# Unread products on TensorE beside the attention units of two lone bodies: the first image's first attention and the last image's second

## The chip, the cores and the metric

The kernel runs on one core of one Trainium2 chip. The metric is the device time of the whole program in microseconds (us); lower is better. What the profile calls PE is TensorE, DVE is VectorE, ACT is ScalarE, POOL is GpSimd, and SP is SyncE, which here only issues plain DMAs. A difference below about 0.5% (23 us) can't be told from no change in this kernel.

## The reference, cut to what matters

Thirty-two images, each of 384 tokens (256 image patches and 128 text tokens) of width 192, go through two layers. Each layer is an attention and a mixture of experts, both with a residual.

```python
h = concat(patch_embedding(x), text_embedding(x_txt))          # 32 x 384 x 192
h = h + L0_attn(layernorm(h))      # 12 heads of 16, softmax, two kinds of queries, values normalised per head
h = h + L0_ffn(layernorm(h))       # 5 experts, all computed, 2 of them weighted in
h = h + L1_attn(layernorm(h))      # 6 heads of 32, causal, low-rank projections
h = h + L1_ffn(layernorm(h))       # 8 experts, each takes up to a fixed number of tokens of the whole batch
```

The change adds nothing to what is computed: its products go to a PSUM bank that nobody reads.

## The kernel before

The program has two stages. `token_stages` takes the images one after the other through everything up to the choice of experts of the second layer. `expert_stage` then runs the eight experts over the tokens of all images. The change touches only the first one.

**Streams and bodies.** The work of one image is cut into four streams: w (embedding and first norm), x (first attention), y (first mixture of experts), z (second attention, and the places of the tokens in the expert buffers). `units()` gives each stream a list of units. The images are pipelined: a body r works on stream w of image r, x of image r-1, y of image r-2 and z of image r-3. `active[r]` says which streams a body has: "w", "wx", "wxy", then "wxyz" for 29 bodies, and at the end "xyz", "yz", "z". So the body "wx" holds the first attention of the first image with no expert work beside it, only a few units of w. The body "z" holds the second attention of the last image, alone. In all the bodies between, products of y stand between the units of attention.

**Order.** `schedule()` merges the streams by strings of letters, `ORDER` and `ORDER_OF_ONE`, and drops units of streams that a body doesn't have. All five engines run through the same list of units, each issuing what is its own; semaphores join them. All is unrolled.

**Units of an attention k** (k = 0 in x, k = 1 in z). "qk" projects a tile of 128 tokens. DVE, POOL and ACT rotate the result and split it into a high and a low part (`parts`). "blocks" transposes the parts on PE (12 transposes) and ACT and DVE copy them to `heads_t`. "maxima" computes two heads' products for one tile of queries in two banks of `bank_v`; DVE reduces each to its row maximum (`neg_max`, L1104). "shift" transposes the maxima and ACT writes them into a row of `heads_t`. "score" computes two heads' shifted scores in two banks of `bank_a`; ACT takes their exponential into `probs` (L760). "apply" multiplies `probs` by the values into `bank_o[k]`, four heads side by side for k = 0, two for k = 1. "sums" and the rest follow.

There are three banks `bank_a`, three `bank_v`, and two `bank_o`, one for each attention. Before it fills a bank, PE waits in `fill_a` or `fill_v` until the bank's last content was read. A first attention has 3 units of blocks, 18 of maxima, 18 of scores and 9 of apply, 48 in all. A second has 3, 9, 9 and 9, 30 in all.

At the start SP also clears `xs_dram` by 29 large DMAs, and POOL gathers the rows of the next image's text tokens (`rows_in`) by indirect DMAs, issued in the unit "rows"; POOL adds the gathered rows into `h[0]` in "patches", and DVE waits for that in the unit "stats" of stream w.

`w_ffn` holds gate and up weights of the first layer's experts as F32R; it is written before the bodies start and isn't changed after.

Of the kernel before, what the change touches and what calls it, by code (L numbers as in the profile page):

```python
# [14 lines left out]
P = 128  # L15
# [198 lines left out]
def token_stages(nc, consts, img, txt, seg, curve, projw, projb, tok_table, seg_table, wqkv,  # L214
# [5 lines left out]
    with ctx:  # L220
        def sb(name, shape, dt=F32):
            return ctx.enter_context(nc.sbuf_tensor(name, shape, dt))

        def ps(name):
            return ctx.enter_context(nc.psum_tensor(name, [P, 512], F32))
# [18 lines left out]
        w_ffn = sb("w_ffn", [P, 3, 2 * E0 * I0 + 8], F32R)  # L244
# [90 lines left out]
        bank_o = [ps(f"bank_o{i}") for i in range(2)]  # L335
# [175 lines left out]
        def body(active, image_w, image_z, fill=()):  # L511
# [58 lines left out]
            with nc.Block(no_gpsimd_drain=True) as block:  # L570
# [209 lines left out]
                def _(pe):  # L780
# [85 lines left out]
                    def apply(k, g, kt):  # L866
# [11 lines left out]
                                           start=(kt == 0), stop=(kt == NT - 1))  # L878
                        mm.then_inc(applied, 1)

                    for r, what, *at in order:
                        if what == "patches":
                            pe.wait_ge(own_ready, nth["w"][r] + 1)
                            for t in range(2):
                                pe.matmul(fill_v("patch", t)[:, 0:D], patches_t[:, t, :], own_proj[:],
                                          start=True, stop=True).then_inc(v_full, 1)
# [16 lines left out]
                        elif what == "qk":  # L903
# [5 lines left out]
                            else:  # L909
# [3 lines left out]
                                          stop=True).then_inc(v_full, 1)  # L913
# [46 lines left out]
                        elif what == "logits":  # L960
# [7 lines left out]
                            for t in range(NT):  # L968
# [4 lines left out]
                                for n, (xb, wb) in enumerate(products):  # L973
                                    mm = pe.matmul(o, ffn_x[:, xb, tile[t]], w_ffn[:, wb, router_cols],
                                                   start=(n == 0), stop=(n == len(products) - 1))
                            mm.then_inc(v_full, 1)
                        elif what == "ffn":
                            e, m = at
                            for name, fill, full in (("gate", fill_a, a_full), ("up", fill_v, v_full)):
                                bank = fill(name, e, m)  # L980
                                first = ffn_cols[name == "up"].start + e * I0 + m * P
                                for n, (xb, wb) in enumerate(products):
                                    mm = pe.matmul(bank[:, 0:T], w_ffn[:, wb, first:first + P], ffn_x[:, xb, :],  # L983
                                                   start=(n == 0), stop=(n == len(products) - 1))
                                mm.then_inc(full, 1)
                        elif what == "down":
                            e, = at
                            pe.wait_ge(hid_ready, hid_nth(r, e, 1) + 1)
                            for t in range(NT):
                                bank = fill_v("down", e, t)  # L990
                                for m in range(2):
                                    mm = pe.matmul(bank[:, 0:D], hid[:, e % 2, m, tile[t]], w_down[:, m, e, :],  # L992
                                                   start=(m == 0), stop=(m == 1))
                                mm.then_inc(v_full, 1)
                        elif what == "low_rank":
                            halves_ready("xt", 2)
                            for w, bank, rows, full in ((w_a, fill_a("r_qk"), 64 + RANK, a_full),
                                                        (w_va, fill_v("r_v"), RANK, v_full)):
                                for half in range(2):
                                    mm = pe.matmul(bank[0:rows, 0:T], w[:, half, :], xt[2][0:KH, half, :],  # L1000
                                                   start=(half == 0), stop=(half == 1))
# [653 lines left out]
```

## Time and profile before

| what | value |
|---|---|
| median of 3 runs | 4603.84 us (4586.52, 4603.84, 4605.22) |
| profiled execution, device time | 4596.28 us |
| its span in the trace | 4594.5 us |
| PE busy over the span | 4277.7 us (93%) |
| DVE, ACT, POOL busy | 62%, 49%, 51% |
| mean granted clock of TensorE | 0.949 of full |

How to read it. The span is the time from the first to the last record of the profiled execution; 1.8 us of its device time lie outside. The granted clock is 1.00 at 2.4 GHz and 0.50 at 1.2 GHz; a stretch with a number between the two has both levels in it. A row of the timeline gives the start and the length of a group of instructions; the length counts to the end of the last one, so the step from one start to the next is what a group costs in a row of work. In brackets stands how long the engine sat idle before the row, and who released it.

### The profile page before, as it was taken

How to read it: one execution, taken by the hardware profiler on the slowest of the kernel's cores; microseconds unless marked ns; L12 is line 12 of the kernel's file. 1: busy time of each engine (PE TensorE's matmuls, PEld its weight loads, DVE VectorE, ACT ScalarE, POOL GpSimd, SP SyncE). 2: the span in 40 equal slices, each digit the busy share in tenths (PEclk: the TensorE clock that was granted, in tenths of full speed). 3: DMA queues.
4: the chain of work that ended last, by engine and by line, in shares of the span. 5: the costliest groups of instructions: out<-in, count | busy, mean ns of one | idle time of the engine just before them, and what ended most of it. 6: DMA issues, size and time to landing. Idle time of an engine off the chain costs nothing. (4 is left out here: it accounts for less than half of the span.)

```text
span 4594.5 us, 77772 instructions
## 1 busy us (share of the span) xinstructions
PE 4277.7 (93%) x26706; PEld 3303.2 (72%) x26706; DVE 2864.9 (62%) x8055; ACT 2257.5 (49%) x5154; POOL 2361.8 (51%) x2439
## 2 busy tenths in 40 slices
PE   2799999999999999999999999999999699999999
PEld 1566666766666666666666667666666489999999
DVE  4476777777777767676767677676775333333333
ACT  1455555555555555555555555555554233333333
POOL 2345555555555555555555555555553245555555
PEclk8799999999999999999999999999999799999999
DMA  8500000000000000000000000000000022222221
GB/s 161 93 8 10 16 9 12 9 12 10 11 11 11 11 11 13 8 13 10 15 11 13 9 12 9 12 9 12 11 9 9 16 70 48 64 74 64 72 63 21
DMA packets 158998, 122.08 MB, mean 27 GB/s; under 512 B 63807, under 2 KB 150358, under 8 KB 158614
## 3 DMA queue, kind: packets, MB, share of 16 engines
q1 hardware_dynamic: 123990, 80.19, 8.1%
q0 software_dynamic: 34624, 36.92, 3.1%
q8 instruction: 223, 3.65, 0.3%
q14 instruction: 161, 1.32, 0.1%
HBM read 76.75 MB, written 74.58 MB: 33 GB/s over the span
## 5 line engine op out<-in xcount | busy, mean ns | idle before, releaser
L760 ACT ACTIVATE probs<-bank_a 128x384 f32<-128x384 f32 (+2 forms) x1728 | 692.0, 453 | 671.0 <-PE bank_a L857 425.8
L1104 DVE TENSOR_REDUCE neg_max<-bank_v 128x1 f32<-128x352 f32 (+3 forms) x1728 | 777.2, 491 | 198.2 <-PE bank_v L832 107.0
L652 POOL TENSOR_SCALAR gate_tanh<-gate_tanh 128x384 f32<-128x384 f32 x320 | 382.2, 1195 | 679.9 <-ACT gate_tanh L777 677.1
L832 PE MATMUL bank_v<-heads_t 50*128 50x352 f32 (+4 forms) x1728 | 402.0, 401 | 77.3 <-DVE neg_max L1104 55.0
L875 PE MATMUL bank_o<-probs,v 128*32 128x384 f32 (+3 forms) x3456 | 441.6, 481 | 4.0 <-ACT sums_t L765 0.3
L832 PEld LDWEIGHTS bank_v<-heads_t 50*128 50x128 f32 (+1 forms) x1728 | 215.1, 194 | 301.3 <-DVE neg_max L1104 142.7
L857 PE MATMUL bank_a<-heads_t 50*128 50x384 f32 (+3 forms) x1728 | 388.2, 386 | 45.3 <-ACT probs L760 38.7
L619 POOL TENSOR_TENSOR rstd<-ve,pow_half 128x3 f32<-128x3 f32 x128 | 113.8, 889 | 578.0 <-DVE ve L1043 576.0
L1406 POOL DMA_INDIRECT out_tokens<-res,token x232 | 230.9, 995 | 331.8 <-DVE res L1592 281.8
L983 PE MATMUL bank_a<-ffn_x,w_ffn 128*128 128x384 f32 x1600 | 389.9, 377 | 0.0
L992 PE MATMUL bank_v<-w_down,hid 128*128 128x192 f32 x1920 | 365.2, 342 | 3.1 <-DVE h_y L1260 1.4
L983 PE MATMUL bank_v<-ffn_x,w_ffn 128*128 128x384 f32 x1600 | 355.7, 355 | 0.0
L654 POOL TENSOR_TENSOR hid<-gate_tanh,hid 128x384 f32<-128x384 f32 x320 | 331.4, 1036 | 33.0 <-DVE hid L1249 7.3
L749 ACT ACTIVATE heads_t<-bank_a 1x384 fp32r<-1x384 f32 x576 | 277.5, 482 | 136.3 <-PE bank_a L845 128.6
L992 PEld LDWEIGHTS bank_v<-w_down,hid 128*128 128x128 f32 x1920 | 318.9, 196 | 35.2 <-issue 31.2
L1585 DVE TENSOR_TENSOR e_hid<-e_bank_v,gated 128x384 f32<-128x384 f32 (+1 forms) x320 | 173.4, 544 | 263.2 <-PE e_bank_v L1471 261.2
L857 PEld LDWEIGHTS bank_a<-heads_t 50*128 50x128 f32 (+1 forms) x1728 | 211.8, 192 | 173.5 <-ACT probs L760 113.5
L1471 PE MATMUL e_bank_a<-split_t,w_in 128*128 128x384 f32 (+1 forms) x1600 | 332.5, 338 | 2.7 <-DVE split_t L1540 2.7
L1249 DVE TENSOR_TENSOR hid<-bank_v,half_gate 128x384 f32<-128x384 f32 x320 | 177.4, 554 | 240.5 <-PE bank_v L983 197.4
L1471 PE MATMUL e_bank_v<-split_t,w_in 128*128 128x384 f32 (+1 forms) x1600 | 325.3, 333 | 0.0
L1442 PE MATMUL e_bank_a<-w_out,e_hid 128*128 128x192 f32 x1856 | 314.8, 326 | 0.5 <-DVE e_hid L1585 0.5
L983 PEld LDWEIGHTS bank_a<-ffn_x,w_ffn 128*128 128x128 f32 x1600 | 286.0, 203 | 39.0 <-issue 24.2
(227 smaller groups left out, 8934.2 us busy)
## 6 DMA issues: line engine op xcount, KB each, us to landing
xs_dram<-zeros SPq DMA_DIRECT2D x29, 780.0 KB, 19.4
rows<-xs_dram SPq DMA_DIRECT2D x232, 96.0 KB
out_tokens<-h_z SPq DMA_DIRECT2D x32, 288.0 KB, 2.3
rows<-xs_dram SPq DMA_DIRECT2D x232, 33.5 KB
raw<-in_w SPq DMA_DIRECT2D x8, 512.0 KB, 3.9
raw<-in_w SPq DMA_DIRECT2D x16, 256.0 KB, 5.2
sofar<-out_tokens,token POOLq DMA_INDIRECT x232
out_tokens<-res,token POOLq DMA_INDIRECT x232
```

The costliest lines, as they stand in the source:

```text
L652: step(pool.tensor_scalar(gate_tanh[:, m, :], gate_tanh[:, m, :], 1.0, None, ALU.add))
L654: pool.tensor_tensor(hid[:, e % 2, m, :], gate_tanh[:, m, :], hid[:, e % 2, m, :], ALU.mult).then_inc(hid_ready, 1)
L749: ins = act.activation(heads_t[k][to:to + 1, b, :], bank[at:at + 1, 0:T], ACT.Copy)
L760: act.activation(probs[:, n % NPROBS, i, lo:T], empty("score", k, g, kt, i)[:, lo:T], ACT.Exp, scale=DHS[k] ** -0.5).then_inc(a_free, 1)
L832: mm = pe.matmul(bank[:, 0:keys], heads_t[k][r:r + rows, b, tile[t]], heads_t[k][r:r + rows, 6 + b, 0:keys], start=True, stop=(k == 0))
L857: mm = pe.matmul(bank[:, lo:T], heads_t[k][at:at + rows, 6 + b, tile[kt]], heads_t[k][at:at + rows, b, lo:T], start=True, stop=(k == 0))
L875: mm = pe.matmul(bank_o[k][i * rows:(i + 1) * rows, lo:T], v[:, kt, PER_GROUP[k] * g + i, :], probs[:, probs_of[r, k, g, kt] % NPROBS, i, ...
L983: mm = pe.matmul(bank[:, 0:T], w_ffn[:, wb, first:first + P], ffn_x[:, xb, :], start=(n == 0), stop=(n == len(products) - 1))
L992: mm = pe.matmul(bank[:, 0:D], hid[:, e % 2, m, tile[t]], w_down[:, m, e, :], start=(m == 0), stop=(m == 1))
L1104: dve.tensor_reduce(neg_max[k][g % 2][:, t, at:at + 1], bank[:, 0:keys], AX.X, ALU.max, negate=True).then_inc(v_free, 1)
L1442: mm = pe.matmul(bank[:, 0:D], hid[:, ch % 2, m, t * P:(t + 1) * P], w_out[ch // NCHUNK % 2][:, m, :], start=(m == 0), stop=(m == NM - 1))
L1471: mm = pe.matmul(bank[:, 0:width], w[:, wb, at:at + P], x[:, xb, 0:width], start=(n == 0), stop=(n == 4))
```

## The change

Ahead of each unit blocks, maxima, score or apply, in the bodies "wx" and "z" alone, PE issues one or two products of a 128 x 128 weight block of `w_ffn` and 512 columns of `w_ffn`, into the one of the two `bank_o` that belongs to the other attention. Two stand ahead of each unit in "wx", one in "z". They wait for nothing, signal nothing, and stand ahead of the unit's own waits.

```diff
+                    def keep_busy(times):
+                        spare = bank_o["z" not in active[r]]
+                        for _ in range(times):
+                            pe.matmul(spare[:], w_ffn[:, 0, 0:P], w_ffn[:, 0, 0:512], start=True, stop=True)
+
                     for r, what, *at in order:
+                        if active[r] in ("wx", "z") and what in ("blocks", "maxima", "score", "apply"):
+                            keep_busy(2 if "x" in active[r] else 1)
                         if what == "patches":
```

What stands in a row on PE in the body "wx", one step of the first attention (apply, two units of maxima, two of scores, apply). L875 is apply, L832 maxima, L857 scores. Before:

```order
L875 MATMUL bank_o0<-probs,v0 32x384 x4
L832 MATMUL bank_v1<-heads_t0 128x352
L832 MATMUL bank_v2<-heads_t0 128x352
L832 MATMUL bank_v0<-heads_t0 128x384
L832 MATMUL bank_v1<-heads_t0 128x384
L857 MATMUL bank_a1<-heads_t0 128x384
L857 MATMUL bank_a2<-heads_t0 128x384
L857 MATMUL bank_a0<-heads_t0 128x384
L857 MATMUL bank_a1<-heads_t0 128x384
L875 MATMUL bank_o0<-probs,v0 32x384 x4
```

The same place on PE after; L884 is the new line.

```order
L875 MATMUL bank_o0<-probs,v0 32x384 x4
L884 MATMUL bank_o1<-w_ffn 128x512 x2
L832 MATMUL bank_v1<-heads_t0 128x352
L832 MATMUL bank_v2<-heads_t0 128x352
L884 MATMUL bank_o1<-w_ffn 128x512 x2
L832 MATMUL bank_v0<-heads_t0 128x384
L832 MATMUL bank_v1<-heads_t0 128x384
L884 MATMUL bank_o1<-w_ffn 128x512 x2
L857 MATMUL bank_a1<-heads_t0 128x384
L857 MATMUL bank_a2<-heads_t0 128x384
L884 MATMUL bank_o1<-w_ffn 128x512 x2
L857 MATMUL bank_a0<-heads_t0 128x384
```

Nothing changes place; five pairs of products come into each such step. In all, 48 pairs stand in the body "wx".

PE in the body "z", one step of the second attention (maxima, score, apply; L838 and L863 add the causal mask), after; before, the same rows stand there without L884.

```order
L884 MATMUL bank_o0<-w_ffn 128x512
L832 MATMUL bank_v0<-heads_t1 128x256
L832 MATMUL bank_v1<-heads_t1 128x256
L838 MATMUL bank_v0<-maskq,identb 128x128
L838 MATMUL bank_v1<-maskq,identb 128x128
L884 MATMUL bank_o0<-w_ffn 128x512
L857 MATMUL bank_a1<-heads_t1 128x256
L857 MATMUL bank_a2<-heads_t1 128x256
L863 MATMUL bank_a1<-maskt,identb 128x128
L863 MATMUL bank_a2<-maskt,identb 128x128
L884 MATMUL bank_o0<-w_ffn 128x512
L875 MATMUL bank_o1<-probs,v1 64x384 x2
```

Here too nothing moves; 30 single products are added. DVE, ACT, POOL and SP have the same instructions in the same order as before.

## Rows read from the trace of the kernel before

**Rows 1.** Stretch: its length, busy PE PEld DVE ACT POOL, PEclk, DMA

```profile
145.00:150.00 5.00, 4.37 (x21) 3.83 (x19) 2.88 (x8) 0.97 (x2) 0.00 (x0) 0.52 1.12 168
```

**Rows 2.** Stretches: the body "wx" from 101 on, then two in body "z"

```profile
101.00:145.00 44.00, 31.57 (x138) 11.59 (x139) 12.53 (x28) 21.01 (x47) 3.52 (x5) 0.50 1.15 174
...
3605.00:3610.00 5.00, 4.97 (x9) 1.88 (x9) 2.33 (x7) 1.46 (x5) 3.08 (x4) 0.50 0.00 0
...
3625.00:3630.00 5.00, 4.88 (x27) 2.59 (x25) 1.78 (x4) 1.98 (x6) 0.00 (x0) 0.70 0.00 0
```

**Rows 3.** What PE waited for, 101 to 145: total us, times, longest

```profile
PE bank_v L832 <- DVE neg_max L1104: 7.3, 6, 3.8
PE bank_a L857 <- ACT probs L760: 6.6, 9, 1.0
PE bank_a L857 <- ACT heads_t L749: 1.1, 1, 1.1
```

**Rows 4.** Timeline of PE in "wx": start, length, line, what [idle before, releaser]

```profile
121.12 0.66 PE L832 MATMUL bank_v<-heads_t 50*128 50x352 f32 x2 [0.74 <-DVE neg_max L1104]
121.55 0.55 PE L857 MATMUL bank_a<-heads_t 50*128 50x384 f32 x2
122.80 0.69 PE L857 MATMUL bank_a<-heads_t 50*128 50x384 f32 x2 [0.70 <-ACT probs L760]
123.42 1.51 PE L875 MATMUL bank_o<-probs,v 128*32 128x384 f32 x8
124.86 0.66 PE L832 MATMUL bank_v<-heads_t 50*128 50x352 f32 x2
126.22 0.69 PE L832 MATMUL bank_v<-heads_t 50*128 50x384 f32 x2 [0.70 <-DVE neg_max L1104]
```

**Rows 5.** Timeline of PE in the body "wxy", clock at 1.00

```profile
199.71 0.43 PE L832 MATMUL bank_v<-heads_t 50*128 50x352 f32 x2
200.84 0.43 PE L832 MATMUL bank_v<-heads_t 50*128 50x352 f32 x2 [0.71 <-DVE neg_max L1104]
201.08 0.37 PE L857 MATMUL bank_a<-heads_t 50*128 50x384 f32 x2
...
237.07 0.45 PE L857 MATMUL bank_a<-heads_t 50*128 50x384 f32 x2 [0.73 <-ACT probs L760]
237.45 0.85 PE L875 MATMUL bank_o<-probs,v 128*32 128x384 f32 x8
238.23 0.44 PE L857 MATMUL bank_a<-heads_t 50*128 50x384 f32 x2
```

**Rows 6.** Timeline of PE at the start of the expert stage, five products a row

```profile
3688.09 1.97 PE L1471 MATMUL e_bank_a<-split_t,w_in 128*128 128x384 f32 x5 [2.66 <-DVE split_t L1540]
3689.85 1.80 PE L1471 MATMUL e_bank_v<-split_t,w_in 128*128 128x384 f32 x5
3691.45 1.69 PE L1471 MATMUL e_bank_a<-split_t,w_in 128*128 128x384 f32 x5
...
3698.04 1.04 PE L1471 MATMUL e_bank_a<-split_t,w_in 128*128 128x384 f32 x5
3698.92 1.04 PE L1471 MATMUL e_bank_v<-split_t,w_in 128*128 128x384 f32 x5
```

**Rows 7.** Timeline of DVE (first row) and POOL around 98 us

```profile
99.61 0.88 DVE L1038 BATCH_NORM_STATS2 st<-h_w 128x6 f32<-128x192 f32 x3 [3.31 <-POOL h_w L613]
...
98.26 0.58 POOL L610 TENSOR_TENSOR segrow<-segrow,cst 128x192 f32<-128x192 f32 x1 [9.13 <-DMA segrow<-in_seg_table,idx]
```

**Rows 8.** Timeline of PE in the body "z"

```profile
3624.95 0.78 PE L832 MATMUL bank_v<-heads_t 96*128 96x256 f32 x2
...
3628.16 0.62 PE L832 MATMUL bank_v<-heads_t 96*128 96x384 f32 x2
...
3632.63 0.50 PE L832 MATMUL bank_v<-heads_t 96*128 96x256 f32 x2
...
3634.57 0.62 PE L832 MATMUL bank_v<-heads_t 96*128 96x384 f32 x2
```

## The prediction

> **What bounds the kernel now.** I began with the shares of busy time: PE is busy 93% of a span of 4594.5 us, so over the whole program TensorE sets the pace. That says nothing of the two bodies that the change touches, so I read those by stretches. From 101 to 145 us, the later part of the first image's first attention, PE works 31.57 of 44 us, at a granted clock of 0.50 the whole time [rows 2]; the clock comes up only at the end of the stretch from 145 to 150, which averages 0.52 [rows 1]. In the body "z" PE is at 0.50 from 3605 to 3610 although it is busy 4.97 of 5 us, and it reaches full clock between 3625 and 3630, where the mean is 0.70 [rows 2]. So both attentions run mostly at 1.2 GHz.
>
> The reader should then see what a step of the first attention is made of at the low clock [rows 4]. From the start of one unit of maxima to the next is 1.36 us (124.86 to 126.22), to the first scores 0.43 (121.12 to 121.55), to the second scores 1.25, to apply 0.62, and from apply to the next maxima 1.44: together 5.10 us. Twice in it PE sits idle for some 0.70 us: it waits for DVE's reduction of a maximum, and for ACT's exponential [rows 3, 4]. In 101 to 145 there are 6 waits of the first kind and 9 of the second, 13.9 us in all, 3.8 us of it a single wait.
>
> **What a pair of added products costs.** The trace has no product of 512 columns, but it has rows of five with 384 columns of the same F32R type and a full weight block [rows 6]. At the low clock five take 1.60 us (3689.85 to 3691.45), 0.32 each; at full clock 0.88 (3698.04 to 3698.92), 0.176 each. By columns, one of 512 is 0.43 us low and 0.235 full, a pair 0.85 and 0.47. The Trainium skill ("TensorE: Matmul & The Clock Gate", section on 56 ns against 53.3) gives 0.216 us for 512 columns at the full clock; a pair would be 0.43, the sum below 0.9 us smaller in "wx", which changes nothing.
>
> **What it gives back.** The same attention stands in the body "wxy" at full clock [rows 5]. Maxima to maxima is 1.13 us there, maxima to scores 0.24, scores to apply 0.38, apply to the next unit 0.78. The work itself takes 0.56 of its time at the low clock, and the waits of 0.71 and 0.73 us stay as they are, for they are DVE's and ACT's time.
>
> **"wx" up to 101 us: nothing.** DVE stands at 99.61 for POOL, and POOL had waited 9.13 us for a gather that landed at 98.26, while the clearing of `xs_dram` fills the queues [rows 7]. Neither is behind PE. DVE's idle of 3.31 us before it is the cover: the six units of maxima ahead are each at most 0.15 us later. If the cover were gone, that would be 1 us.
>
> **"wx" from 101 to 145.** The 31.6 us of PE work would take 17.7 at full clock: 13.9 us less. Against it, 38 of the 48 units lie here (11 maxima, 18 scores, 9 apply) with a pair each, 38 x 0.47 = 17.9 us. Sixteen of the pairs lie in a wait of at least 0.64 us (the sixteen that are listed in [rows 3]), which hides 7.5 us. Exposed are 10.4 us. The net is -3.5 us if the clock is full throughout. It won't be: PE still has the hole before 101, and a clock that was down stays down for a while when dense work begins; in the expert stage that starts at 3688.09 the products are still slow at 3691.45 and fast at 3698.04 [rows 6]. I take one step of the attention at the low clock with pairs. Three of its five units have no wait before them, so it is 5.10 + 3 x 0.85 + 2 x 0.15 = 7.95 us, against about 5.0 for a step at full clock with pairs (1.13 + 0.24 + 1.05 + 0.38 + 0.78 and three pairs exposed; the 1.05 is 1.25 less what 0.46 us of work saves): +3.0 us. The stretch comes to -0.5.
>
> **After 145 us.** The transposes of the sums, the norm and the attention output run at the low clock until shortly before 150 [rows 1]. PE is busy 4.37 of 5 us there. With the clock already up that is 0.44 x 4.4 = 1.9 us less; DVE's division lies between the transposes, so I take -1.5. After that, a hole waits for POOL and the clock is as before. "wx" together: **-2 us**.
>
> **"z".** Eleven of its 30 units lie before the clock comes up and nineteen behind. At the low clock one product is 0.43 us; some five of the eleven are not covered by a wait: +2.3. Behind, fifteen of nineteen are exposed: 15 x 0.235 = +3.5. The gain is only what comes from an earlier rise. A step of maxima, scores and apply of the same shapes is 3.21 us at the low clock (3624.95 to 3628.16) and 1.94 at the full (3632.63 to 3634.57) [rows 8]. If the clock rises some 5 us earlier, that is 1.3 for this step and about as much for the rest: -2.5. "z" together: **+3 us**, from -2 (rise at the first transposes) to +6 (no earlier rise).
>
> **Sum.** -2 + 3 = +1 us on a profiled execution of 4596.3 us, that is 4597. The runs shown have their median 7.6 us above this execution, so I name 4604. Everything is far below the 23 us (0.5%) that a measurement of this kernel can tell from no change.
>
> **Rivals.** One: *the clock stays low in "wx" in spite of the products.* For it: PE was busy 4.97 of 5 us at 0.50 [rows 2]. That PE is busy doesn't bring the clock up by itself. Against it: those products fill only a part of the array, while the rows after which the clock did rise are of full 128 x 128 blocks [rows 6], as the added ones are. Then 22 pairs are exposed at 0.85 us, 18.7, the other sixteen at 0.15, 2.4, and nothing is given back: +21 us, with +6 in "z" +27, 4631 us. It decides from the point at which a step stays at 7.95 us: each that does costs 3 us more than one at the full clock, and with eight of them the time is 0.5% above the median. The same page of the Trainium skill (section "What's actually happening") says that sustained activity releases the throttle; by that the rival would not occur, but the row of 4.97 us at 0.50 is against taking it as sure.
>
> Two: *the clock rises but falls back, or rises late,* since the added products are short and the waits remain. Each step at the low clock costs 3 us against the full one, so three more are +9: with "z" at its upper end -2 + 9 + 6 = +13, 4617.
>
> Three: *the clock is up all the time from the first transposes of "blocks",* since two products stand ahead of these too. That spares the slow step (-3), and the rise in "z" at its transposes turns +3 into -2: together -7, 4597. Speaks for it: nothing but small holes between the transposes. Against: the hole of several us in which PE waits for `h_w` [rows 7].
>
> Four: the change doesn't do what it says. The list of PE's instructions shows 96 and 30 products, so only a clock that doesn't care is left, which is rival one.
>
> **How the numbers follow.** Forecast (4598 to 4609) 0.66, rival two 0.14, rival three 0.14, rival one 0.06. The runs before spread from 4586.5 to 4605.2 with the same program, and the median may fall anywhere in such a spread, so the range is 4588 to 4620: it takes in rivals two and three and leaves rival one out. Faster by over 0.5% would need -23 us, more than all that both stretches could give if the pairs were free (13.9 + 1.9 + 5): 0.03. Slower by over 0.5% is rival one and some of the spread: 0.05. No difference 0.92.
>
> **What would show it.** In the profile after, the granted clock between 105 and 145 us is near 1.00 (rival one: 0.50; two: 0.6 to 0.8). The step from apply to apply with both maxima in it is near 5.0 us, as now. The new line has 126 products. PE's idle time before L832 and L857 falls to about 0.25 us a wait. The maximum at 101 us still begins when POOL's addition of the gathered rows is done. The body "z" ends no earlier than before, measured from its start. The prediction is wrong if the step is clearly shorter than 4.5 us, if exposed pairs cost much more than 0.47, or if the time moves in a stage where no product was added.

## The result and the profile after

The changed kernel takes 4610.33 us (median of 12 runs, 4598.31 to 4615.94). The kernel before, in the same comparison, takes 4591.64 us (12 runs, 4585.39 to 4605.22). The ratio is 1.0034, 95% interval 1.0023 to 1.0045: 16 us slower, between 11 and 21 (the two medians lie 19 apart; below I go by the ratio). That is inside the 0.5% that I had called no difference, and inside the range, but it has a sign, and I had forecast none. The median of three that stood ahead of the prediction, 4603.84, was 12 us above the one that more runs give.

The page of the profile after, first lines: the clock is a little higher than before (0.952 against 0.949), and PE is busy 40 us longer.

```profile
span 4614.1 us, 78024 instructions
...
PE 4317.5 (94%) x26832; PEld 3322.6 (72%) x26832; DVE 2869.3 (62%) x8055; ACT 2259.6 (49%) x5154; POOL 2366.3 (51%) x2439
```

The stretches of the body "wx" after (columns as in [rows 1]), which answer to [rows 2]:

```profile
105.00:110.00 5.00, 5.00 (x12) 2.23 (x12) 2.53 (x7) 0.86 (x2) 0.00 (x0) 0.50 1.13 176
...
120.00:125.00 5.00, 5.00 (x18) 2.13 (x19) 0.00 (x0) 1.70 (x4) 0.00 (x0) 0.50 1.11 187
125.00:130.00 5.00, 4.90 (x23) 2.24 (x25) 1.91 (x4) 3.56 (x8) 0.00 (x0) 1.00 1.13 190
```

PE is busy without a gap, and still stays at 1.2 GHz until 125 us. Then it is at 2.4 GHz to the end of the attention. With the products the clock comes up 25 us earlier than in the profile before, but 16 us later than the 109 that one slow step from 101 on would have given.

The timeline of PE at the low clock and at the full one (start, length, line, what), which answers to [rows 4] and [rows 5]; L884 is the added line:

```profile
113.07 1.51 PE L875 MATMUL bank_o<-probs,v 128*32 128x384 f32 x8
114.51 1.22 PE L884 MATMUL bank_o<-w_ffn 128*128 128x512 f32 x2
115.66 0.66 PE L832 MATMUL bank_v<-heads_t 50*128 50x352 f32 x2
116.25 1.22 PE L884 MATMUL bank_o<-w_ffn 128*128 128x512 f32 x2
117.40 0.69 PE L832 MATMUL bank_v<-heads_t 50*128 50x384 f32 x2
...
122.70 1.51 PE L875 MATMUL bank_o<-probs,v 128*32 128x384 f32 x8
...
129.82 0.85 PE L875 MATMUL bank_o<-probs,v 128*32 128x384 f32 x8
130.60 0.73 PE L884 MATMUL bank_o<-w_ffn 128*128 128x512 f32 x2
131.27 0.44 PE L832 MATMUL bank_v<-heads_t 50*128 50x384 f32 x2
131.64 0.73 PE L884 MATMUL bank_o<-w_ffn 128*128 128x512 f32 x2
132.44 0.43 PE L832 MATMUL bank_v<-heads_t 50*128 50x352 f32 x2
...
135.67 0.85 PE L875 MATMUL bank_o<-probs,v 128*32 128x384 f32 x8
```

The reader should read steps from start to start. From apply to apply is 9.63 us at the low clock (113.07 to 122.70) and 5.85 at the full one (129.82 to 135.67); before it was about 5.1 at the low clock. A pair of products takes 1.15 us low (114.51 to 115.66) where I had 0.85, and 0.67 to 0.80 full (130.60 to 131.27; 131.64 to 132.44, with a short wait at its end) where I had 0.47. The unit behind it got longer too: two products of maxima take 0.59 us (115.66 to 116.25) and took 0.43 before [rows 4]; at the full clock 0.36 (132.44 to 132.80) against 0.24 [rows 5]. Even at twice the clock, the attention with pairs is slower than without them at half of it.

**Where the time went.** The two executions can be compared piece by piece. In the body "wx" from the first transposes of the norm (PE, `xn_w`) to those of the attention's sums, and on to the first maxima behind the hole of the next body; in "z" from the transposes of `xn_y` to those of the sums and on to those of `xn_z`. These are the rows of PE of the kernel before at the five places:

```profile
60.95 0.87 PE L805 MATMUL bank_a<-ident,xn_w 128*96 128x128 f32 x3 [16.10 <-DVE xn_w L1200]
...
144.62 2.18 PE L939 MATMUL bank_v<-ident,sums_t 128*128 128x128 f32 x9 [0.61 <-ACT sums_t L765]
...
187.74 0.66 PE L832 MATMUL bank_v<-heads_t 50*128 50x352 f32 x2 [7.45 <-DVE neg_max L1104]
...
3593.84 0.87 PE L805 MATMUL bank_a<-ident,xn_y 128*96 128x128 f32 x3 [7.33 <-DVE xn_y L1200]
...
3652.49 0.94 PE L805 MATMUL bank_a<-ident,xn_z 128*96 128x128 f32 x3 [3.43 <-DVE xn_z L1200]
```

and after:

```profile
60.38 0.87 PE L805 MATMUL bank_a<-ident,xn_w 128*96 128x128 f32 x3 [16.07 <-DVE xn_w L1207]
...
156.76 1.20 PE L946 MATMUL bank_v<-ident,sums_t 128*128 128x128 f32 x9 [0.61 <-ACT sums_t L765]
...
198.35 0.66 PE L832 MATMUL bank_v<-heads_t 50*128 50x352 f32 x2 [7.47 <-DVE neg_max L1111]
...
3609.92 0.88 PE L805 MATMUL bank_a<-ident,xn_y 128*96 128x128 f32 x3 [7.33 <-DVE xn_y L1207]
...
3671.98 0.94 PE L805 MATMUL bank_a<-ident,xn_z 128*96 128x128 f32 x3 [3.43 <-DVE xn_z L1207]
```

"wx" to its sums went from 83.67 to 96.38 us, +12.7, and to the next body's maxima from 126.79 to 137.97, +11.2: behind the attention 1.5 us come back, where the transposes run at the full clock. "z" to `xn_z` went from 58.65 to 62.06, +3.4. Together +14.6, close to the measured 16. The 3400 us between (198.35 to 3609.92) differ by 5.5 us, though nothing in them was changed. The profiles of the nine kernels below show what that is: over all eleven, the same unchanged piece takes 3393 to 3412 us, without relation to what was added elsewhere. So a difference of two spans says little here, and the pieces say more. They have a scatter of their own: "wx" came out 1.0 shorter in e2, which adds nothing there, and the same 30 single products made "z" longer by 1.5 (e2) to 3.4 us (the change).

### The profile page after: what moved, and what is told of

Read it like the earlier page. It is cut to its first block and busy times, and to the rows that moved or that the text cites. A ratio compares the mean times of both kernels' runs of the same rounds, so it can differ in the third digit from the quotient of the medians.

```text
span 4614.1 us, 78024 instructions
## 1 busy us (share of the span) xinstructions
PE 4317.5 (94%) x26832; PEld 3322.6 (72%) x26832; DVE 2869.3 (62%) x8055; ACT 2259.6 (49%) x5154; POOL 2366.3 (51%) x2439
## 5 line engine op out<-in xcount | busy, mean ns | idle before, releaser
L832 PE MATMUL bank_v<-heads_t 50*128 50x352 f32 (+4 forms) x1728 | 398.8, 399 | 67.0 <-DVE neg_max L1111 46.2
L875 PE MATMUL bank_o<-probs,v 128*32 128x384 f32 (+3 forms) x3456 | 437.8, 476 | 3.7 <-ACT sums_t L765 0.2
L832 PEld LDWEIGHTS bank_v<-heads_t 50*128 50x128 f32 (+1 forms) x1728 | 214.4, 193 | 292.2 <-DVE neg_max L1111 135.9
L857 PE MATMUL bank_a<-heads_t 50*128 50x384 f32 (+3 forms) x1728 | 384.8, 382 | 37.6 <-ACT probs L760 32.4
L857 PEld LDWEIGHTS bank_a<-heads_t 50*128 50x128 f32 (+1 forms) x1728 | 210.5, 190 | 167.6 <-ACT probs L760 105.1
```

The costliest lines, as they stand in the source:

```text
L832: mm = pe.matmul(bank[:, 0:keys], heads_t[k][r:r + rows, b, tile[t]], heads_t[k][r:r + rows, 6 + b, 0:keys], start=True, stop=(k == 0))
L857: mm = pe.matmul(bank[:, lo:T], heads_t[k][at:at + rows, 6 + b, tile[kt]], heads_t[k][at:at + rows, b, lo:T], start=True, stop=(k == 0))
L875: mm = pe.matmul(bank_o[k][i * rows:(i + 1) * rows, lo:T], v[:, kt, PER_GROUP[k] * g + i, :], probs[:, probs_of[r, k, g, kt] % NPROBS, i, ...
```

## The experiments

In the table stand, for each kernel, the time against the kernel before (ratio x 4592 us, with its 95% interval) and the change of the pieces in its profile: "wx" from the norm's transposes to the next body's maxima, "z" from `xn_y` to `xn_z`.

| kernel | measured, us | "wx" | "z" | sum of the two |
|---|---|---|---|---|
| the change | +16 (+11 to +21) | +11.2 | +3.4 | +14.6 |
| e1: pairs in wx only | +7 (+3 to +12) | +11.3 | 0.0 | +11.3 |
| e2: singles in z only | +3 (-3 to +8) | -1.0 | +1.5 | +0.5 |
| e3: 8 columns for 512 | +26 (+18 to +33) | +13.4 | +14.0 | +27.4 |
| e4: rows in holes only | +3 (-1 to +8) | -1.9 | +5.3 | +3.4 |
| e5: one each in wx | +25 (+19 to +32) | +17.0 | +3.2 | +20.2 |
| e6: a row first, then pairs | +11 (+3 to +18) | +3.0 | +3.2 | +6.2 |
| e7: e3 in bf16 | +20 (+13 to +26) | +5.0 | +11.4 | +16.4 |
| e8: the change in bf16 | +12 (+6 to +18) | +3.7 | -1.2 | +2.5 |
| e9: rows in other holes | -2 (-6 to +2) | +0.1 | 0.0 | +0.1 |

In nine of the ten the sum of the two pieces lies in the interval of the measurement; in e8 it doesn't, and that stays open (below). Each profile is of one execution; that of the change is the longest of its twelve.

### e1 and e2: one body each

```diff
-if active[r] in ("wx", "z") and what in (...)
+if active[r] in ("wx",) and what in (...)      # e1;  ("z",) in e2
```

> Only the 96 products of the body wx; the 30 of the body z are left away. My reading of the two traces is that wx is 10.6 us longer (the rows of the first norm's transposes behind the attention begin at 157.80 against 146.60, and the next body's first maxima behind its hole at 198.35 against 187.74), z 1.5 us in its attention and 1.9 behind it, and the rest is drift between two executions. By that: +10 us, between +7 and +13. Rival, that the products of z or something that they do to what follows carry the loss: under +5 us.

> Only the 30 products of the body z. By my reading +3 us, between 0 and +6. By the rival (loss outside the bodies with products) over +8 us.

e1 measured +7 (ratio 1.0016, 1.0006 to 1.0027), e2 +3 (1.0006, 0.9994 to 1.0017). Both lie in what the first theory expects. The rival, a loss that comes from "z" or from outside the bodies, wanted e1 under +5 and e2 over +8. e1's interval, +3 to +12, doesn't exclude the first; e2's, which ends at +8, speaks against the second. The pieces decide: +11.3 and 0.0 in e1, -1.0 and +1.5 in e2. The body "wx" carries most.

### e3: products without columns

```diff
-pe.matmul(spare[:], w_ffn[:, 0, 0:P], w_ffn[:, 0, 0:512], start=True, stop=True)
+pe.matmul(spare[:, 0:8], w_ffn[:, 0, 0:P], w_ffn[:, 0, 0:8], start=True, stop=True)
```

> All 126 products at the same places, with the same 128 x 128 weight block, but 8 columns instead of 512. They do next to no work in the array, so the clock should come up no earlier than before (0.50 until about 150 us). If a product costs what its columns take, 126 of them cost under 2 us. If each change to and from a full block costs extra (the pair of maxima took 0.59 us instead of 0.43 and a pair of products 1.15 instead of 0.85), that extra is left: 22 exposed units at about 0.4 us in wx and 20 in z at 0.2, +8 to +13 us.

It measured +26 (1.0056, 1.0039 to 1.0072), with e5 the largest loss of all and twice what I expected. Here products that stream 8 columns cost more than products that stream 512: the intervals of the two times meet (+18 to +33, +11 to +21), but the pieces are clear, +27.4 against +14.6. PE's timeline of e3:

```profile
112.64 0.59 PE L884 MATMUL bank_o<-w_ffn 128*128 128x8 f32 x2
113.16 0.66 PE L832 MATMUL bank_v<-heads_t 50*128 50x352 f32 x2
113.75 0.59 PE L884 MATMUL bank_o<-w_ffn 128*128 128x8 f32 x2
```

A pair takes 0.52 us (112.64 to 113.16), of which 16 columns are 0.013. The unit behind it is at 0.59 (113.16 to 113.75), as in the changed kernel. And nothing lifts the clock:

```profile
100.00:145.00 45.00, 38.90 (x154) 23.93 (x154) 13.85 (x34) 15.52 (x35) 3.99 (x6) 0.50 1.14 171
...
3600.00:3640.00 40.00, 34.34 (x125) 21.57 (x126) 12.19 (x29) 10.79 (x25) 6.42 (x10) 0.50 0.00 1
```

In "z" the attention before the change got to 0.70 between 3625 and 3630 by itself [rows 2]; with narrow products between its own it stays at 0.50 to the end of the body. That is the part which I hadn't expected: 14 us in "z". So a foreign product has a fixed price besides that of its columns. And in "wx" the clock came up at 125 us with products of 512 columns, but only at 160, behind the attention, with those of 8.

### e7 and e8: what the fixed price is

```diff
-pe.matmul(spare[:, 0:8], w_ffn[:, 0, 0:P], w_ffn[:, 0, 0:8], ...)
+pe.matmul(spare[:, 0:8], identb[:], onesb[:, 0:8], ...)                         # e7, bf16
-pe.matmul(spare[:], w_ffn[:, 0, 0:P], w_ffn[:, 0, 0:512], ...)
+pe.matmul(spare[:].rearrange("p (a n) -> p a n", n=P), identb[:],               # e8, bf16
+          onesb[:].unsqueeze(1).to_broadcast([P, 4, P]), ...)
```

In the cuts above e7 is set against e3, and e8 against the change.

> 126 narrow products (8 columns) at the same places, but with a bf16 weight block. If the extra of a narrow product is its weight load (0.333 us a load of F32R, 0.147 of bf16 at the low clock in the rows), the loss shrinks with it, from +25 us to about +11. If the extra is the change to and from a product on all rows (the two products of a unit run side by side on different rows and no longer do), it stays near +25.

> The change with bf16 operands: 512 columns, 126 products, a bf16 weight block. By the weight load theory each unit is some 0.15 us cheaper at the low clock: +8 to +11 us instead of +16. By the other theory as the change, +16. If bf16 products of ones and zeros don't bring the clock up, wx stays at 0.50 and the loss is over +20.

PE's timeline of e7:

```profile
119.87 0.22 PE L884 MATMUL bank_o<-onesb,identb 128*128 128x8 bf16 x2
120.02 0.69 PE L857 MATMUL bank_a<-heads_t 50*128 50x384 f32 x2
120.64 0.22 PE L884 MATMUL bank_o<-onesb,identb 128*128 128x8 bf16 x2
```

The pair takes 0.15 us instead of 0.52 (119.87 to 120.02), so 0.37 of the fixed price of a pair goes with the type F32R, which I put down to its two weight loads. The unit between (0.62, 120.02 to 120.64, for scores) is as long as in e3. That is the other part of the price, which both theories left open, and it depends on neither type nor columns. The kernel before has the same two lengths without any added product:

```profile
103.23 0.69 PE L857 MATMUL bank_a<-heads_t 50*128 50x384 f32 x2 [0.64 <-ACT probs L760]
103.69 0.55 PE L832 MATMUL bank_v<-heads_t 50*128 50x384 f32 x2
```

A unit of 384 columns takes 0.46 us when another unit of products on 50 rows follows (103.23 to 103.69), and 0.62 when apply follows, whose products take 128 rows (122.80 to 123.42 in [rows 4]). So 0.16 us is what a unit loses when the next products are not of its kind. Ahead of apply it was lost before too; the pairs make it so behind every unit.

In "wx" the loss fell from +13.4 to +5.0. Measured, e7 is at +20 (1.0043, 1.0029 to 1.0056), between the two expectations, and its interval, +13 to +26, still holds the +25: the clock of "z" stays low here too, +11.4.

The median weight load of the added products in e3 takes 333 ns:

```profile
L884 PEld LDWEIGHTS bank_o<-w_ffn x126: 190/333/339, 69.4 to 3659.5; 128*128 128x128 f32 x126
```

The Trainium skill ("TensorE: Matmul & The Clock Gate", section on weight-path perf modes) says that weights of 128 columns load faster when they aren't fp32. The rows agree: 333 ns in F32R, 147 ns for the bf16 block of the mask (L838, in "z" of the kernel before), and in e7 itself a median of 118 ns, over both levels of the clock. The same page (section "Step-by-step") says that PE pulls the next weight load ahead of running products. Here that holds inside a row of alike products (0.32 us for 384 columns at the low clock, [rows 6]) but not on the way to or from the units: a wide pair of 0.85 us of columns takes 1.15.

e8, the change in bf16, came out at +12 (1.0026, 1.0013 to 1.0039), just above the +8 to +11 expected and below the change's +16, but the intervals overlap. Its profile is better than that, +3.7 in "wx" and -1.2 in "z":

```profile
111.49 1.04 PE L884 MATMUL bank_o<-onesb,identb 128*128 128x512 bf16 x2
112.45 1.31 PE L875 MATMUL bank_o<-probs,v 128*32 128x384 f32 x8
...
123.62 0.60 PE L884 MATMUL bank_o<-onesb,identb 128*128 128x512 bf16 x2
124.15 0.85 PE L875 MATMUL bank_o<-probs,v 128*32 128x384 f32 x8
```

A pair takes 0.96 us at the low clock and 0.53 at the full one, against 1.15 and 0.67 in the change. But here the clock also came up at 113 us and not at 125, so the two can't be told apart in the +3.7. Whether the rise came as early in the other executions, and what the remaining 9 us are, I can't say.

### e5: one product instead of two

```diff
-keep_busy(2 if "x" in active[r] else 1)
+keep_busy(1)
```

> One product ahead of each unit of wx instead of two (z as in the change). What I now hold is that the first product of a unit pays its weight load in full, some 0.3 us at the low clock beside the 0.43 us of its columns, that the second pays little more than its columns, and that a rise of the clock gives back less than the products take. Then a unit costs 0.72 instead of 1.15 us at 0.50 and some 0.45 instead of 0.75 at full clock. If the clock comes up at about the same time as with two (125 us), wx is 10 x less than 1 us a step better: +3 to +6 us in wx, +5 to +9 in all. If one product is not enough to bring the clock up in wx, all 9 steps are at about 7.3 us instead of 5.1 and wx is +16 or more, +18 in all.

It measured +25 (1.0055, 1.0041 to 1.0070), worse than two, and beyond both expectations. PE's timeline shows the clock come up and go again inside the attention:

```profile
112.26 1.51 PE L875 MATMUL bank_o<-probs,v 128*32 128x384 f32 x8
...
119.89 1.51 PE L875 MATMUL bank_o<-probs,v 128*32 128x384 f32 x8
...
121.88 0.71 PE L884 MATMUL bank_o<-w_ffn 128*128 128x512 f32 x1
122.52 0.43 PE L832 MATMUL bank_v<-heads_t 50*128 50x352 f32 x2
...
126.10 0.79 PE L884 MATMUL bank_o<-w_ffn 128*128 128x512 f32 x1
126.82 1.51 PE L875 MATMUL bank_o<-probs,v 128*32 128x384 f32 x8
```

A unit is 0.36 us long at 122.52 (full clock), and apply takes 1.44 us again at 126.82 (low). One product each didn't hold the clock here; nearly all steps ran at 1.2 GHz with 7.6 us instead of 5.1 (112.26 to 119.89 from apply to apply). "wx" is +17.0, as the second expectation had it (+16 or more).

### e6: the row first

```diff
+started = False
 for r, what, *at in order:
+    if (active[r], what, *at) == ("wx", "maxima", 0, 2, 1):
+        keep_busy(8)
+        started = True
-    if active[r] in ("wx", "z") and what in (...):
+    if (started and active[r] == "wx" or active[r] == "z") and what in (...):
```

> No products in wx before the eighth unit of maxima; there eight in a row, in the hole in which PE waits for the first norm of the next image, and from that unit on the pairs as in the change. z as in the change. It asks how much of the loss of wx is the 23 us that it ran at 0.50 with the pairs in place (a step of 9.63 us, against 5.85 at full clock and 5.15 before). If the row brings the clock up by about 102 and the pairs hold it, steps are 5.85 us from the start: six times +0.7, three times +0.2, -1.6 behind: wx +3 us, +5 to +7 in all. If the row doesn't bring it up: as the change, +14 to +17.

It measured +11 (1.0023, 1.0007 to 1.0039); the interval holds the +5 to +7 and the +14 to +17 of the other expectation. The profile is on the first: "wx" +3.0, where +3 was expected, and the step is that of the full clock early on:

```profile
122.48 0.85 PE L875 MATMUL bank_o<-probs,v 128*32 128x384 f32 x8
...
128.33 0.85 PE L875 MATMUL bank_o<-probs,v 128*32 128x384 f32 x8
```

So in these two profiles 8 of the 11 us that the change costs in "wx" come from the two steps that it runs at the low clock with the pairs in place. (e6 also leaves out the pairs ahead of its row, but its first scores start no earlier: 42.87 us behind the norm's transposes, 42.12 in the change.) The other 3 are made up so: the first scores start 1.8 later than before (42.87 against 41.09), the steps with pairs take 2.7 longer even at the full clock (88.20 to the sums, less 42.87, against 83.67 less 41.09), and 1.5 come back behind them. One reservation: the eleven times of e6 lie in two groups, six from 4591 to 4601 us and five from 4610 to 4620, and the profile is that of the shortest. Whether the row brought the clock up in the others, no profile shows.

### e4 and e9: rows in holes, nothing beside the units

```diff
+in_holes = {("wx", "maxima", 0, 0, 1): 16, ("wx", "maxima", 0, 2, 1): 10,        # e4
+            ("z", "xt", 2): 28, ("z", "xt", 3): 12}
+in_holes = {("wxy", "xt", 1): 14, ("wxy", "maxima", 0, 0, 1): 28}                # e9
+keep_busy(in_holes.get((active[r], what, *at), 0))
 # e9, expert stage, ahead of its first transposes
+for _ in range(12):
+    pe.matmul(bank_v[3][:, 0:P], ident[:], ident[:], start=True, stop=True)
```

> No product beside the units; instead 16 and 10 in a row in the two holes of wx in which PE waits for DVE (ahead of the second and of the eighth unit of maxima), and 28 and 12 in two holes of z (ahead of the transposes of its first and of its last norm). If the clock is what the products are good for and it holds once it is up, the attention of wx takes about 30 us from 101 on instead of 43, and z about 10 us less: -15 to -25 us. If it falls back as soon as the products end, because the work of wx at full clock leaves PE idle for more than half of the time, the gain is a few us in z alone: -3 to -8 us.

> No product in the bodies wx and z. Rows of products in holes behind which dense work runs at 0.50: 14 ahead of the transposes of the first expert layer's input in wxy (hole of 3.5 us, behind it 13 us at 0.50), 28 ahead of the second unit of maxima in wxy (hole of 7.5 us, behind it 6.5 us at 0.50), and 12 products of 128 columns of F32 at the start of the expert stage, while PE waits for its first rows (behind it 9 us at 0.50). If a row of products pays only where it costs nothing and where PE-bound work follows: -4.5, -1.5 and -2.5 us, -8 in all, between -12 and -4. If the clock falls between a row and the work as it did in the attention of wx, no difference.

e4 measured +3 (1.0007, 0.9997 to 1.0017): no gain, and outside both expectations. The products fit into the holes, and the clock comes up behind them, but the attention's own work doesn't hold it:

```profile
100.00:105.00 5.00, 3.22 (x18) 1.81 (x17) 4.19 (x14) 1.74 (x4) 3.08 (x5) 1.00 1.14 178
105.00:110.00 5.00, 2.95 (x18) 1.35 (x18) 3.63 (x9) 2.51 (x6) 0.43 (x1) 0.67 1.17 157
110.00:115.00 5.00, 4.29 (x19) 1.68 (x19) 1.16 (x3) 2.90 (x7) 0.00 (x0) 0.50 1.09 195
```

From 101.82 to 106.79 the steps ran at 2.4 GHz, PE idle for 2 of 5 us, and the clock fell. The gain in "wx" is 1.9 us, little more than the 1.0 that e2 shows with nothing added there. In "z" the projections ran at full clock, and then the attention stayed at 0.50 to its end, where before it had risen on its way, so the body lost 5.3 us.

e9 measured -2 (0.9996, 0.9986 to 1.0005): no difference that can be told. Locally one sees why: the row in the first hole shortened the dense rows behind it from 6.36 us (before, 167.61 to 173.97) to 5.13, but PE then waits for DVE's maxima, and that wait ends at the same time as before (+0.1 us). The row in the second hole gave some 0.6 us behind it: from the first maxima to the first ones behind the shift it is 11.3 us (186.97 to 198.31), before 12.0 (187.74 to 199.71).

```profile
166.81 1.95 PE L991 MATMUL bank_a<-ffn_x,w_ffn 128*128 128x384 f32 x5
...
171.94 0.46 PE L931 MATMUL bank_a<-identr,parts 128*128 128x128 f32 x4
```

The products at the start of the expert stage ended 4 us before the rows arrived, and the clock was at 0.50 when the dense work began. No version of these beats the kernel before.

## Why the prediction was right or wrong

**What bounds the two bodies: right.** PE ran at half clock in both, and the waits between units are DVE's and ACT's.

**The price of a pair: too low.** I scaled rows of five alike products by columns, to 0.85 and 0.47 us. Inside such a row the weight load is hidden; beside a unit it isn't, and the unit itself gets 0.16 us longer at the low clock and 0.12 at the full one, a term that the sum left out. The kernel before held it already: 0.62 us from scores to apply in [rows 4], 0.46 in the row shown under e7. A covered unit costs nothing more at the full clock (maxima to maxima is 1.13 us after, 125.47 to 126.60, as in [rows 5]). At the low clock it is not covered: 1.74 us (115.66 to 117.40) against 1.36, where I had allowed 0.15. So a step at the low clock was 9.63 us, forecast 7.95, and at the full 5.85, forecast 5.0. At the full clock the pairs eat up the whole gain of the clock and 0.7 us a step more. e6 shows what this term does by itself: with the clock up from the first steps on, the steps and what lies behind them were +1.2 in its profile (+2.7 and -1.5), where the forecast's terms give -5 (-3.5 and -1.5).

**One step at the low clock: too few.** The clock came up at 125 us; one step from 101 on would have been about 109. By the start of the second apply (122.70 against 112.31 before, 62.32 us behind the norm's transposes against 51.36) the change had lost 11.0 of its 12.7 us. e6 shows it apart: with the clock up from the start of the steps, 8 us of it are gone. This was rival two, "rises late", to which I gave 0.14, at the price of 3 us a step against one at the full clock; it was over two steps at 3.8 us each (9.63 - 5.85), or 4.5 against a step of the kernel before.

**What the rise behind gives: right in size, but not the products' own.** 1.5 us were forecast, 1.5 measured (12.7 to 11.2). In e2, which adds nothing in "wx", the clock came up at 145 us and not shortly before 150 as in the profile before, and the same 1.5 us are there (+0.5 to the sums, -1.0 to the next body's maxima). Its transposes of the sums, which took 2.18 us before:

```profile
145.32 1.20 PE L946 MATMUL bank_v<-ident,sums_t 128*128 128x128 f32 x9 [0.61 <-ACT sums_t L765]
```

**Before 101 us: nearly.** DVE's and POOL's wait for the gather covered most: the first scores start 42.12 us behind the norm's transposes (102.50 - 60.38), before 41.09 (102.04 - 60.95), the 1 us that I had named as the price without cover. Half of it, 0.5, is also there in e2, which adds nothing here.

**"z": the number right, its terms not.** +3 forecast, +3.4 in the profile, of which 1.5 are in the attention. The other 1.9 lie behind it, where the clock fell before the output projection; e2's profile, with the same products, has nothing there. e2 alone measured +3, with an interval that holds zero. The attention began 16 us later on the program's time than before, and its clock went like this:

```profile
3630.00:3635.00 5.00, 4.01 (x27) 2.68 (x25) 2.23 (x6) 1.92 (x4) 0.94 (x2) 0.95 0.00 0
3635.00:3640.00 5.00, 3.89 (x18) 3.11 (x19) 1.75 (x5) 1.22 (x3) 0.00 (x0) 0.73 0.00 0
3640.00:3645.00 5.00, 5.00 (x31) 3.00 (x30) 1.78 (x4) 1.72 (x6) 0.00 (x0) 0.93 0.00 0
```

It came up some 20 us behind the transposes of `xn_y`, in the unit blocks, where before it took 34 (3628 less 3593.84); it fell once for some 3 us and rose again. I had reckoned with a rise 5 us earlier, worth 2.5; it was 14, less the 3 of the fall. At the same rate that gives back more than 5 us, and as the attention still grew by 1.5, its products cost some 7 us by this estimate, and not 5.8. The two errors offset each other, so the agreement is partly luck. (Five products at 0.43 are 2.2 us, too, not the 2.3 of the sum.)

**The rule that busy brings the clock up.** The prediction's rival one held a row of 4.97 us at 0.50 against it, and the forecast gave too little weight to it. After, PE was busy 5.00 of 5 us from 100 to 125 at 0.50. The Trainium skill ("TensorE: Matmul & The Clock Gate", section "What's actually happening") says that activity releases the throttle; by these stretches, being busy in the profile is not enough. e3 bears this out from the other side: in 40 us of "z" (from 3607.3 on) PE was busy 35.99 us at 0.50, and before, in the same place (from 3600 on), 32.73 us at 0.65. What made the clock rise at 125 and not earlier, no run here shows; that stays open.

**The level.** I forecast 4604 around a median of three runs. More runs of the kernel before have it at 4592, and the change at 4610. The range held, from 4588 to 4620, but by luck: set around 4592, as it would have been with more runs, it ends at 4608.

## What to carry to other kernels

Products that only keep TensorE's clock up have to be paid in the coin of the stage: price one at the place where it will stand, with its weight load exposed and with the neighbour's loss of overlap, not from a row of alike ones. Where the work between two waits is short, twice the clock halves only that work, and one foreign product per unit can cost more than this (e5). Before adding any, look whether the stage's own work would hold the clock (e4) and whether the time saved ends in a wait for another engine (e9).

## What the runs showed of the hardware

Between two units at the low clock a pair of products of 8 columns on a full F32R weight block took 0.52 us (e3), and 0.15 on a bf16 block (e7); the 16 columns are 0.013 of it. Two products of 50 rows and 352 columns that stand side by side on different rows take 0.43 us when more of their kind follow, and 0.59 when products on all rows follow, whatever their type or length; at 384 columns 0.46 and 0.62. The second length is that of two products one behind the other (at the low clock 384 columns take 0.32 us in [rows 6]), so I take the difference as overlap with the unit behind. The time of the clock's rise varies between executions of the same instructions: in the first attention without products it was shortly before 150 us in the profile before, 145 in e2 and 153 in e9. Narrow products beside a second attention kept TensorE at 1.2 GHz to its end (e3, e7), where before the clock rose at 3628 us. And the 3400 us that no kernel of this study altered took from 3393 to 3412 us in their profiles.
